# Attention's probabilities turned by DMA in halves instead of by TensorE in fp32, in a decoder layer with experts

## What is computed

```python
x = layernorm(x + attn(x))            # self-attention, 16 heads of 64, no mask, biases on q, k, v and the output
x = layernorm(x + xattn(ctx, x))      # cross attention, one head of 64, scores + mask * -1e9
x = layernorm(x + ffn(x))             # 32 experts of width 384, top 8 with shared weights, silu(gate) * up
# attn: att = softmax(q @ k.T / 8); out = (att @ v) @ Wo.T + bo
```

## Time and profile before

| | us |
|---|---|
| median of 3 runs (lowest, highest) | 2281.71 (2278.87, 2300.57) |
| the profiled execution's own time | 2282.65 |
| its span, first to last instruction | 2280.9 |
| TensorE busy | 2102.4 |
| VectorE busy | 1332.4 |
| ScalarE busy | 1198.7 |
| GpSimd busy | 1078.6 |
| mean granted TensorE clock | 0.949 of full |

### The profile page before, as it was taken

One profiled execution on the slowest core, in us unless ns is written; L12 is line 12 of the kernel. 1 busy time (PEld: TensorE's weight loads), 2 busy tenths in 40 slices (PEclk: granted clock), 3 DMA queues, 4 the chain that ended last, 5 costly groups with the idle time before them and its releaser, 6 DMA issues.

```text
span 2280.9 us, 43549 instructions
## 1 busy us (share of the span) xinstructions
PE 2102.4 (92%) x15590; PEld 1296.5 (57%) x15590; DVE 1332.4 (58%) x2409; ACT 1198.7 (53%) x2878; POOL 1078.6 (47%) x863
## 2 busy tenths in 40 slices
PE   7899999999999999999999976999999999999990
PEld 5566666666666666676666643444444544444440
DVE  5556567567567576666656664555455545554534
ACT  6765665565565665675565541434443444344334
POOL 3454444454454454444444531455555555555522
PEclk9999999999999999999999987999999999999995
DMA  6021011011011011011101003777777777777739
GB/s 200 32 76 52 20 34 53 18 33 51 18 33 51 18 36 48 18 51 33 37 32 33 28 34 100 198 172 202 173 171 182 196 171 170 193 184 170 174 45 313
DMA packets 114600, 219.74 MB, mean 96 GB/s; under 512 B 14576, under 2 KB 37104, under 8 KB 114544
## 3 DMA queue, kind: packets, MB, share of 16 engines
q1 hardware_dynamic: 85600, 148.73, 18.9%
q0 software_dynamic: 28944, 70.27, 16.6%
HBM read 158.67 MB, written 60.29 MB: 96 GB/s over the span
## 4 chain that ended last, share of the span: by engine, by line
PE 75%; DVE 11%; issue 6%; ACT 5%; POOL 1%; DMA 1%; DVEq 0%; SPq 0%; ACTq 0%; POOLq 0%
PE bank L472 48%; PE bank L782 11%; PE bank L536 4%; PE bank L548 3%; ACT arena_p L857 3%; PE bank L771 3%; PE bank L510 2%; PE bank L666 2%; DVE s_max L1116 2%; DVE x L1163 2%; ACT arena_wo L1076 1%; DVE stage L1283 1%; PE bank L639 1%; POOL arena_p L1535 1%; PE bank L482 0%
## 5 line engine op out<-in xcount | busy, mean ns | idle before, releaser
L472 PE MATMUL bank<-arena_v,arena_wo 128*128 128x512 f16 x2304 | 502.5, 379 | 0.9 <-PE bank L673 0.9
L1535 POOL TENSOR_TENSOR arena_p<-arena_p,s_rden 128x1024 f32<-128x1024 f32 x128 | 246.0, 1922 | 435.7 <-DVE s_rden L1124 435.7
L472 PE MATMUL bank<-xt,arena_wo 128*128 128x256 f16 x3072 | 394.5, 290 | 4.8 <-DVE arena_wo L1086 4.6
L472 PEld LDWEIGHTS bank<-arena_v,arena_wo 128*128 128x128 f16 x2304 | 225.2, 98 | 273.3 <-PE bank L673 1.5
L472 PEld LDWEIGHTS bank<-xt,arena_wo 128*128 128x128 f16 x3072 | 308.9, 104 | 85.0 <-issue 31.8
L1635 POOL DMA_INDIRECT acc_rows<-arena_wo,cur_to x128 | 202.1, 1579 | 310.0 <-ACT arena_wo L1056 278.7
L857 ACT ACTIVATE arena_p<-bank,s_neg 128x256 f32<-128x256 f32 x512 | 235.4, 472 | 181.3 <-DVE s_neg L1119 181.3
L1086 DVE SCALAR_TENSOR_TENSOR arena_wo<-stage,arena_wo 128x3072 f16<-128x3072 f32 (+2 forms) x74 | 182.3, 2465 | 182.9 <-ACT arena_wo L929 174.9
L1086 DVE SCALAR_TENSOR_TENSOR arena_v<-bank,arena_v 128x512 f16<-128x512 f32 x192 | 129.5, 688 | 233.8 <-ACT arena_v L867 143.0
L782 PE MATMUL bank<-arena_wo 128*128 128x512 f16 x1152 | 264.2, 379 | 0.7 <-DVE arena_wo L1477 0.7
L1629 POOL DMA_INDIRECT arena_p<-x_rows,cur_from x128 | 216.8, 1694 | 56.4 <-issue 29.3
(11 more groups left out here) (159 smaller groups left out, 3064.4 us busy)
## 6 DMA issues: line engine op xcount, KB each, us to landing
stage<-wguT SPq DMA_DIRECT2D x32, 1536.0 KB, 8.7
stage<-wdnT SPq DMA_DIRECT2D x32, 768.0 KB, 10.0
xt<-xT SPq DMA_DIRECT2D x16, 512.0 KB, 4.1
xr<-x_rows SPq DMA_DIRECT2D x16, 512.0 KB, 3.9
stage<-ctxT SPq DMA_DIRECT2D x16, 512.0 KB, 4.7
x_rows<-x SPq DMA_DIRECT2D x16, 512.0 KB, 2.8
acc_rows<-x SPq DMA_DIRECT2D x16, 512.0 KB, 3.7
arena_wo<-acc_rows SPq DMA_DIRECT2D x8, 1024.0 KB, 10.8
```

Of the source, the lines that this page charges most:

```text
L472: mm = pe.matmul(out_ap, lhs(a, i), rhs(c, i), start=(n == 0 and i == 0), stop=(n == 2 and i == chunks - 1))
L1535: gp.tensor_tensor(rows, rows, s_rden[:, j % 2, :].unsqueeze(2).to_broadcast([P, 4, S]), ALU.mult)\
```

## The change

- `exps` no longer sums rows; the exponent gets log 4096 added (through `maxima`), so the probabilities come out unnormalised and scaled. Scores have two banks per pair parity (`ps_s`), so four in all.
- The probabilities are split before they are turned: ScalarE copies the high half (`probs_hi`), GpSimd subtracts (`probs_lo`), and SP issues one DMA transpose per head, 128x1024 of 16 bits, into a ring of four pairs that lies in `stage` (`turn_probs`).
- `weigh` takes the turned probabilities as weights and the values as moving columns, 64 and a column of ones per head (`HV`), so queries are on partitions and the row sum is in column 64. VectorE divides (`heads_out`); every second pair GpSimd splits (`heads_parts`) and SP transposes both pairs of heads (`turn_heads`).
- The value bias is taken through the output weights once (`bias_through`, `bias_row`).
- The rounds have a new order on every engine; keys, queries and scores of cross attention move to the round after the tail, the choice of experts to the round after that; the last rounds are no longer cut short. Expert 0's weights are loaded in round 16 and expert 1's after both halves of expert 0 are converted; SP's rounds are written out instead of looped.
- `hot_low` and `hot_high` are laid out with the one-hot axis innermost.

```diff
-            def turn(b, j):
-                pe.wait_ge(p_done, count(b, EC, j + 1))
-                past(pe, pt_lo, count(b, 2 * EC, 2 * j))
...
             def weigh(b, j):
-                past(pe, o_hi, count(b, EC, j))
+                past(pe, o_done, count(b, EC, j))
...
+                pe.wait_ge(p_turned[j % PT], count(b, 2 * 32, 32 * (j // PT + 1)))
+                for t in range(TT):
+                    for h in range(2):
+                        for n, (a, c) in enumerate(((0, 0), (1, 0), (0, 1))):
+                            for i in range(2):
+                                mm = pe.matmul(ps_o[:, 2 * t + h, :], pT[:, j % PT, h, 4 * c + 2 * t + i, :],
+                                               v[:, a, i, 2 * j + h, :], start=(n == 0 and i == 0), stop=(n == 2 and i == 1))
                 mm.then_inc(pv_mm, 1)
...
+            def turn_probs(b, j):
...
+                past(sp, pv_mm, count(b, EC, j + 1 - PT))
+                for h in range(2):
+                    sp.wait_ge(p_lo, count(b, 2 * EC, 2 * j + h + 1))
+                    sp.dma_start_transpose(pT[:, j % PT, h], halves[:, j % 2, h].rearrange("p s n -> p (s n)"))\
+                      .then_inc(p_turned[j % PT], 16)
+
+            def turn_heads(b, j):
+                if j % 2:
+                    if j == 1:
+                        past(sp, wo_mm, count(b, TT))
+                    sp.wait_ge(o_lo, count(b, EC // 2, j // 2 + 1))
+                    sp.dma_start_transpose(oT[:, j // 2], o_rows[:, :, :, :, :].rearrange("p j s t n -> p (j s t n)"))\
+                      .then_inc(o_turned, 16)
...
             def exps(b, j):
-                past(act, t_mm, count(b, 2 * EC, 2 * j - 2))
+                past(act, p_lo, count(b, 2 * EC, 2 * j - 2))
...
+            def probs_hi(b, j):
+                for h in range(2):
+                    waits_apart(act, s_const, N_CONST,
+                                (p_turned[(j - 2) % PT], count(b, 2 * 32, 32 * ((j - 2) // PT + 1))),
+                                (e_done, count(b, 2 * EC, 2 * j + h + 1)))
+                    nc.scalar.activation(halves[:, j % 2, h, 0, :], probs[:, j % 2, h].rearrange("p t k -> p (t k)"),
+                                         ACT.Copy).then_inc(p_hi, 1)
...
+            def heads_out(b, j):
+                past(dve, o_lo, count(b, EC // 2, j // 2))
+                dve.wait_ge(pv_mm, count(b, EC, j + 1))
+                vec.reciprocal(s_rden[:, j % 2, :], ps_o[:, :, DK]).then_inc(o_rden, 1)
+                wait_apart(dve, o_rden, count(b, EC, j + 1), s_constv, N_CONSTV)
+                vec.tensor_tensor(o32[:, j % 2, :].rearrange("p (g d) -> p g d", g=4), ps_o[:, :, 0:DK],
+                                  s_rden[:, j % 2, :].unsqueeze(2).to_broadcast([P, 4, DK]), ALU.mult).then_inc(o_done, 1)
...
+            def probs_lo(b, j):
+                for h in range(2):
+                    pool.wait_ge(p_hi, count(b, 2 * EC, 2 * j + h + 1))
+                    gp.tensor_tensor(halves[:, j % 2, h, 1, :], probs[:, j % 2, h].rearrange("p t k -> p (t k)"),
+                                     halves[:, j % 2, h, 0, :], ALU.subtract).then_inc(p_lo, 1)
...
-                vec.tensor_tensor(hot_low[:, :, :], low_no[:, :, :],
-                                  low_neg[:, :].unsqueeze(1).to_broadcast([P, LOW, TT * NX]), ALU.is_equal).then_inc(rt, 1)
...
+                vec.tensor_tensor(hot_low[:, :, :], low_no[:, :].unsqueeze(1).to_broadcast([P, TT * NX, LOW]),
+                                  low_neg[:, :].unsqueeze(2).to_broadcast([P, TT * NX, LOW]), ALU.is_equal).then_inc(rt, 1)
```

More of the change, by code:

```diff
@@ L362, in piece, with columns @@
             def piece(n, src):
+                for dst, one in src:
+                    sp.dma_start(dst, one).then_inc(piece_sem(n), 16)
+            def columns(n):
+                w, at, width = PIECES[n]
                 if n >= 4:
@@ new lines, in turn_heads, with steps @@
+            def turn_heads(b, j):
[5 more added lines that the diff above has]
+                      .then_inc(o_turned, 16)
+            def steps(r, first, last):
+                pair = pairs(r, r < B, 0 < r <= B)
+                for s in range(first, last):
+                    pair(turn_heads, s - 5)
+                    pair(turn_probs, s - 2)
@@ L435, in _ @@
+            for r in range(B):
+                first_half(r)
+                if r == 0:
+                    cross_pieces()
+                if r + 1 < B:
+                    load_x(r + 1)
+                second_half(r)
+            first_half(B)
+            second_half(B)
+            first_half(B + 1)
+            second_half(B + 1)
+            first_half(B + 2)
+            sp.wait_ge(ew_lo_gu, 1)
+            sp.wait_ge(ew_lo_dn, 1)
+            load_expert(1, 0)
             sp.wait_ge(slot_mm, B)
@@ L514, in scores, with values @@
                 mm.then_inc(s_mm, 1)
-            def values(b, g, tail, fill):
+            def values(b, g, route, fill):
                 half, t = g // 2, g % 2
@@ L682, in step @@
                     pair(scores, s - 2)
-                    pair(turn, s - 3)
                     for on, run in between:
@@ L686, in step @@
                             run()
-                    pair(weigh, s - 4)
                     if head:
                         qk_pair(b, s)
-                last = last_tail(r)
-                late_fill = isinstance(r, int) and r == B + 1
-                if isinstance(r, int) and r == B + 2:
-                    fill_slots(f)
+                    pair(weigh, s - 4)
+                drain = isinstance(r, int) and r > B
+                if drain and not route:
+                    positions(f, head, route)
@@ L699, in work @@
                 if head:
-                    values(b, 0, tail, fill)
-                step(1, [(route, lambda: cross_turn(u))])
+                    values(b, 0, route, fill)
+                step(2, [(fill, lambda: positions(f, head, route))])
+                if head:
+                    values(b, 1, route, fill)
                 if route:
-                    cross_weigh(u)
-                if head:
-                    values(b, 1, tail, fill)
-                step(2, [(route, lambda: cross_project(u, 0))])
@@ L740, in work @@
-                if head:
-                    values(b, 3, tail, fill)
-                step(6, [(tail, lambda: turn_x1(t, 0, head, route, fill)), (route, lambda: positions(u))])
-                if late_fill:
-                    keep_warm(WARM_ROUTE[4])
-                if tail:
-                    turn_x1(t, 1, head, route, fill)
-                step(7, [(tail, lambda: ctx_kv(t)), (tail, lambda: cross_q(t))])
-                if tail:
-                    cross_scores(t)
+                if tail:
+                    project(t, 0, head, fill)
@@ L947, in work, with step, queries @@
                 pair = pairs(r, head, tail)
-                def step(s, between=(), first=(), late=()):
-                    pair(turned_hi, s - 3)
-                    for on, run in first:
-                        if on:
-                            run()
-                    pair(exps, s - 2)
-                    for on, run in between:
-                        if on:
-                            run()
-                    if s != 4:
-                        pair(heads_out, s - 4)
-                    for on, run in late:
-                        if on:
-                            run()
-                    if head and s < EC - 1:
+                def step(s):
+                    pair(exps, s - 2)
+                    pair(probs_hi, s - 2)
+                def queries(s):
+                    if head:
                         qk_out(b, s)
+                drain = isinstance(r, int) and r > B
+                if drain and not route:
+                    return
                 if head and not (isinstance(r, int) and r == 0):
@@ L1570, in work, with step @@
                 pair = pairs(r, head, tail)
[L1572 to L1580 removed]
+                def step(s, between=()):
+                    pair(qk_low, s - 1)
+                    for on, run in between:
+                        if on:
+                            run()
+                    pair(heads_parts, s - 5)
+                    pair(probs_lo, s - 2)
                 step(0)
```

689 lines of the change are left out of this document (339 added, 350 removed).

## The result

| | before | after |
|---|---|---|
| median (lowest, highest), 20 runs each | 2277.47 (2270.08, 2300.57) us | 2294.47 (2270.84, 2325.55) us |
| predicted | | 2253 us |

The ratio is 1.0051 [1.0026, 1.0076]: slower by 0.5%, within what a measurement of this kernel tells from no change. It leaves out executions over 1.5% above the fastest of their kernel, five of after's 20; the ratio of the medians in the table is 1.0075. The forecast was a gain of 1.3%. The profiled execution of after, span 2315.5 us, is one of its longer ones.

The account below looks back on a forecast made before the run. TensorE was taken as the bound. Rounds 3 to 15 at -32, rounds 0 to 2 at -18 and the drain at +22 made -28 on 2282.65 us: 2254.5, as a median 2253 us; range 2130 to 2400.

Parts of the forecast that it names:

- rounds 3 to 15: The 13 rounds with all parts: a gain of 2.5 us each, -32 us in all.
- rounds 0 to 2: First three rounds, without tell: they lose the turns and gain the bias row, -18 us (0 to -25).
- drain: Between the attention rounds and the experts: more serial work and a later first expert, +22 us (0 to +40).
- the sum of a round: TensorE's round after the change: 65.5 us of work, 12.0 of waits and 2.5 for the clock, 80.0 us.
- (c): Rival: TensorE's waits eat all the gain, 17 us in place of 12, a round of 83, 2292 us; chance 0.20.
- The new wait: TensorE's cross_weigh waits each round for turned2_lo, behind tell on VectorE: 5.0 us (3.6 to 6.7).
- The small waits: TensorE's other waits in a round, on results of other engines, 0.6 to 1.2 us each.
- 82.5 us: Length of a round before the change, from the same TensorE wait six rounds apart.
- Transposes: SP's 20 DMA transposes of 256 KB a round: 2.7 us to landing each, 54 us a round, not the bound.
- Rival (a): Transposes in SP's queue bound the round, from 4.1 us each; at 5 us each 2584 us; chance 0.20.
- The clock: Time TensorE loses in a round to a lower granted clock: 2.5 us taken, 2.2 before the change.
- Rival (b): tell hides and the small waits halve: a round of 70.0 us, 2124 us; chance 0.18.

Follow-up runs that it names:

- e5_shifted: The kernel after with 70 matmuls of 32 columns added at its start, its rounds untouched: 2266.62 us.
- e1_unrolled: The kernel after with TensorE's rounds 4 to 15 written one after another in place of a loop: 2266.23 us, ratio 0.9977.
- e3_plain_copies: The kernel after with each of the 320 transposing DMAs replaced by a plain DMA of the same 256 KB: 2296.27 us.
- e6_drain: e1_unrolled with expert 0's low-half conversions moved earlier on VectorE in the last rounds, and load_expert(1) ahead of the last store of w32: 2250.36 us.
- e8_hole: e6_drain with tell moved to where VectorE and GpSimd were idle, and fill_slots and add_slots moved too: 2174.23 us, ratio 0.959.

## Why the prediction was wrong, and where it was right

The stages of `e5_shifted`, after without the fetches, against before, by three marks of the traces: the first scores of round 16 (1319.05 before, 1268.00), the start of the experts (1427.46 and 1407.16), the end.

| part | forecast | measured |
|---|---|---|
| rounds 3 to 15 | -32 | 13 x (80.7 - 83.8) = -40 |
| rounds 0 to 2 | -18 | -51 + 40 = -11 |
| drain | +22 | 139.2 - 108.4 = +31 |
| sum at the experts' start | -28 | -20 |
| fetches at the loop's jump | 0 | +55 in the profiled execution, about +28 in the median |
| experts and end | 0 | 853.4 - 853.4 = 0 |

**The step that failed** is the sum of a round: "Work after: 74.9 - 7.5 - 1.9 = 65.5 us", with its waits and the clock, took TensorE's instructions as always at hand. The rounds' sum missed 6.3 us at each of eight jumps (87.1 us a round with the fetch, 80.8 without). I counted 32 matmuls a round more as 0.78 us a pair, and never as instructions in a loop. Nor was it among the rivals: (c), 2292 us with a chance of 0.20, gives after's time almost exactly, but that is luck: its cause, 17 us of waits on other engines, did not come (they were about 12), and by its own terms its round is 65.5 + 17 + 2.5 = 85 us and not 83.

The fetches are not the whole miss. Without them the change is still no gain that the runs tell from none: `e1_unrolled` has 0.9977 [0.9947, 1.0006] and `e5_shifted` 1.0008 [0.9961, 1.0056] against the kernel before. In the table the drain is 9 us over its term and rounds 0 to 2 are 7 over theirs; there my own terms, 19.7 of turns less 5.3 for the biases, come to -14 and not -18.

**Its terms.** Weighing 0.72 to 0.73 us start to start (0.78 taken): the 24 loads hide. `fill_slots` 1.69 (1.8). The new wait 5.15 (5.0), here with what makes it (VectorE's timeline):

```profile
763.61 0.69 DVE L1135 SCALAR_TENSOR_TENSOR arena_v<-bank,arena_v 128x512 f16<-128x512 f32 x1 [4.08 <-ACT arena_v L913]
764.22 2.28 DVE L1343 TENSOR_TENSOR stage<-low_no,low_neg 128x2048 f16<-128x2048 f16 x1
766.42 1.22 DVE L1345 TENSOR_TENSOR stage<-high_no,high_one 128x1024 f16<-128x1024 f16 x1
...
768.55 0.68 DVE L1135 SCALAR_TENSOR_TENSOR p2T<-bank,p2T 128x512 f16<-128x512 f32 x1
```

`tell` is 4.3 us (4.2). In the earlier trace rows the first compare took 1.23 with GpSimd idle, here 2.28 with GpSimd idle, so the input that now repeats innermost costs the double speed; the sentence of the Trainium skill ("VectorE: DVE Perf Modes", Mode 2x_1P) holds on its second half too. The small waits were placed less well: `positions` 1.5 (0.6), values 3 1.2 (0.9), `weigh` about once or twice a round with up to 1.7 (1.0 and 0.6), `cross_project` none (1.0), `cross_scores` 0.2 to 0.6 (1.0).

**A before that was too fast.** 82.5 us came from 721.97 to 1217.09. The same wait stands at 212.51 and 1302.32: 83.8 for 13 rounds. The stretch held four rounds of 81.7 to 81.9, where the others take 83.3 to 85.3. One of either kind, in windows:

```profile
636.65:721.97 85.32, 79.93 (x722) 55.89 (x723) 54.87 (x114) 51.15 (x151) 39.29 (x30) 0.94 0.11 34
887.36:969.21 81.85, 78.11 (x723) 55.33 (x723) 52.95 (x114) 51.15 (x151) 39.16 (x30) 0.96 0.11 36
```

The same matmuls take 3.5 us more at a granted clock of 0.94 than at 0.96, and no instruction packet is near. Twelve rounds of the one or the other kind would be 42 us apart (an estimate), about as far as the kernel before's own runs, 2256 to 2303 us beside the experiments. So a wide spread alone is no sign of fetches. By my own 80.0 and this 83.8 the first term would have been -49.

**Transposes.** SP's issue of one takes 1.28 us and it lands 3.2 us after (2.7 taken); 20 in a round are 26 us of SP and at most 64 of the queue. The rows of line 433 (x, min/median/max ns):

```profile
L433 SPq DMA_TRANSPOSE stage<-arena_p x256: 1231/1282/3652, 30.0 to 1340.6; - x128
...
DMA to landing us min/median/max: 3.0/3.2/7.5
```

Plain copies of the same size in `e3_plain_copies`: 0.46 and 2.3 us. Rival (a) is dead, and of the two sentences of the Trainium skill neither price holds: not 0.7 us, nor as fast as a plain copy ("Advanced Engine Details and Errata", X-Bar Transpose (TRN2)), nor 10.5 for eight blocks one by one ("VectorE: DVE Perf Modes", the three transpose paths).

**The drain** grew by 31 us where I had 22. The late load of expert 1 (issued 1441.3, converted 1454.8 to 1457.5) is there as argued, but `e6_drain` shows it to be worth 6.5 us and not 11. The other 24 are the serial part, for which I took 10: TensorE waits 7.9 and 6.8 us in it for the tables that `tell` builds (`e5_shifted`, at 1305.85 and 1355.27), where the kernel before waits 0.4.

**The clock.** I took 2.5 us a round for it. From `e6_drain` to `e8_hole` a round loses 6.3 us. Waits of 5.15 and 1.2 became 0.81 (`cross_weigh`), 0.85 (`cross_project`) and 1.05 (projection 0): 3.6 us of it. Most of the other 2.7 is the clock: 24 matmuls at 2.79 in place of 4.1, 12 at 2.76 in place of 4.3 (in two rounds of three). Rival (b), a round of 70 with `tell` hidden, did not come in after; where `e8_hole` hides it by moving three calls, a round is 74.6.

## What to carry to other kernels

A loop on TensorE of some 1570 instructions, weight loads counted, can be fetched again at its jump back; one of 1508 was not: before judging a change that adds matmuls to such a loop, compare the instruction queue's packets inside it, and unroll it if they return (a shift helped here, but another shift brought them). A moved call is paid by what is queued behind it on its engine, so look in the timeline for a stretch where its engine is idle, GpSimd too (beside which VectorE's compares took 4.03 us in place of 2.28), and TensorE has one long group; moving it by a few lines only hands the wait to the next customer. And take a round's length over all rounds, not over the stretch on the screen.

## What the hardware showed beyond what was expected

- At a jump back, TensorE's loop of 1570 instructions was fetched again in 8 of 11 cases, nine packets of 16,384 bytes, with waits of 3.5 to 5.1 and 2.0 to 2.9 us. 70 tiny matmuls ahead of it ended that; 58 of them brought it to a kernel that had none. The first packet starts 0.2 to 0.5 us after TensorE stops. Why nine packets come for a body of 6.1 pieces I can't explain.
- A compare of 2048 elements of 16 bits takes 1.23 us, 2.28 with an input that repeats innermost, and 4.03 where GpSimd works beside it, whose own 1.16 us become 3.21.
- A transposing DMA of 256 KB takes 1.28 us to issue on SP and lands after 3.2, a plain one 0.46 and 2.3.
- The kernel before has rounds of 85.3 and of 81.8 us with the same work, at granted clocks of 0.94 and 0.96.
